# Linear attention with a mixture of experts: the queries projected transposed, for two chunks at once

## What is computed

```
h = _layernorm(x, axis=-1) * (1 + ca) + sa
q = _heads(x @ wq.T);  k = _heads(x @ wk.T);  v = _heads(x @ wv.T)
def _phi(x, omega):
    proj = jnp.einsum('bhnd,md->bhnm', x, omega)
    norm = 0.5 * jnp.sum(x * x, axis=-1, keepdims=True)
    return jnp.exp(proj - norm) / math.sqrt(M)
kv_cumsum = jnp.cumsum(jnp.einsum('bhnm,bhnd->bhnmd', phi_k, v), axis=2)
out = jnp.einsum('bhnm,bhnmd->bhnd', phi_q, kv_cumsum)
z = 1.0 / (jnp.einsum('bhnm,bhnm->bhn', phi_q, k_cumsum) + 1e-06)
x = x + ga * ((out * z[..., None]) @ wo.T + bo)
x = x + gb * ffn(_layernorm(x) * (1 + cb) + sb)
```

## Time and profile before

| | |
|---|---|
| three runs | 727.18, 728.42, 729.02 us; median 728.42 |
| the profiled execution | 727.18 us, its span 725.1 us |
| TensorE (PE) busy | 697.4 us, 96% |
| VectorE (DVE) busy | 536.0 us, 74% |
| ScalarE (ACT) busy | 387.6 us, 53% |
| GpSimd (POOL) busy | 335.6 us, 46% |

### The profile page before, as it was taken

The page is one execution under the profiler, slowest core; times in us unless marked ns, Lnnn a source line. Parts: engine busy times, 40 slices in busy tenths (PEclk is TensorE's granted clock), DMA queues, the critical chain, the costliest instruction groups (busy, mean ns, idle before and its releaser), DMA issues. The chain is left out here.

```text
span 725.1 us, 27349 instructions
## 1 busy us (share of the span) xinstructions
PE 697.4 (96%) x11452; PEld 604.1 (83%) x11452; DVE 536.0 (74%) x1685; ACT 387.6 (53%) x740; POOL 335.6 (46%) x625
## 2 busy tenths in 40 slices
PE   8999999999999999999999999999999789999956
PEld 8788888888888888888888888888887779999942
DVE  6687888878878887888878878888775456565416
ACT  5755566665656665666656566665552144544310
POOL 3002545555544445454545554545447306556550
PEclk9999999999999999999999999999999999999989
DMA  9974000000000000000000000000000154553128
GB/s 252 362 268 178 11 9 11 10 9 11 14 15 10 11 10 11 10 10 11 9 11 11 14 14 9 11 11 11 10 11 14 49 177 130 168 173 113 51 82 304
DMA packets 32705, 47.25 MB, mean 65 GB/s; under 512 B 4132, under 2 KB 20168, under 8 KB 32584
## 3 DMA queue, kind: packets, MB, share of 16 engines
q1 hardware_dynamic: 23296, 32.62, 13.4%
q0 software_dynamic: 4096, 8.42, 3.6%
q10 hardware_dynamic: 5192, 4.47, 1.9%
HBM read 22.21 MB, written 23.36 MB: 63 GB/s over the span
## 5 line engine op out<-in xcount | busy, mean ns | idle before, releaser
L1297 POOL DMA_INDIRECT y_rows<-y_sb,row_id x64 | 62.8, 982 | 66.0 <-DVE y_sb L1442 49.9
L1108 POOL DMA_INDIRECT dispatched<-h_cur,slot x64 | 67.3, 1051 | 17.8 <-issue 16.1
L1376 ACT ACTIVATE hidden<-bank,b_col 128x512 f32<-128x512 f32 x64 | 43.3, 689 | 58.2 <-PE bank L1348 57.8
L632 ACT ACTIVATE phi_k<-expo_k 128x1024 f32<-128x1024 f32 x32 | 33.9, 1058 | 74.5 <-DVE expo_k L768 70.7
L648 ACT COPY v_sb<-bank 128x512 f32<-128x512 f32 x64 | 37.6, 587 | 62.1 <-PE bank L279 58.7
L527 PEld LDWEIGHTS bank<-woT,attT 128*128 128x128 f32 x512 | 61.9, 192 | 3.2 <-ACT attT L738 0.6
L859 DVE TENSOR_TENSOR scores<-bank,within 128x512 f32<-128x512 f32 x64 | 41.2, 686 | 31.2 <-PE bank L310 31.2
L527 PE MATMUL bank<-woT,attT 128*128 128x128 f32 x512 | 62.4, 275 | 0.4 <-ACT attT L738 0.4
L1317 PE MATMUL bank<-w_sb,hidden 128*128 128x128 f32 x512 | 59.7, 275 | 0.8 <-issue 0.8
L137 POOL TENSOR_TENSOR rs<-var,power 128x1 f32<-128x1 f32 x64 | 37.1, 579 | 49.8 <-DVE var L132 49.5
L1317 PEld LDWEIGHTS bank<-w_sb,hidden 128*128 128x128 f32 x512 | 58.3, 192 | 1.2 <-issue 1.2
(11 more groups left out here) (243 smaller groups left out, 2037.9 us busy)
## 6 DMA issues: line engine op xcount, KB each, us to landing
dispatched<-blank SPq DMA_DIRECT2D x16, 524.0 KB, 3.1
region<-dispatched SPq DMA_DIRECT2D x30, 262.0 KB, 2.9
y_rows<-blank SPq DMA_DIRECT2D x8, 512.0 KB, 3.9
w_nat<-in_L_ffn_w_dram SPq DMA_DIRECT2D x8, 256.0 KB, 3.7
y_got<-y_rows SPq DMA_DIRECT2D x8, 256.0 KB, 6.8
y_got<-y_rows ACTq DMA_DIRECT2D x8, 256.0 KB, 7.4
out_dram<-x_sb SPq DMA_DIRECT2D x8, 256.0 KB, 3.7
w_sb<-in_L_ffn_w_dram ACTq DMA_DIRECT2D x6, 256.0 KB, 2.8
```

The source lines that it names most:

```text
L1108: pool.indirect_dma_start(out=dispatched[:, :], in_=h2_cur[par][:], in_offset=None, out_offset=bass.IndirectOffsetOnAxis(ap=slot[par][:, k ...
L1297: pool.indirect_dma_start(out=y_rows[:, :], out_offset=bass.IndirectOffsetOnAxis(ap=row_id[par][:, t:t + 1].bitcast(U32), axis=0), in_=y_s ...
L1376: act.activation(hidden[par][:, k, :], psum[2 + k][:], ACT.Gelu, bias=b1_col[:, bass.ds(e * KH + k, 1)]).then_inc(sem(f"hid{k}_out"), 1)
```

## The change

The queries are no longer projected by rows and then transposed. `project_qT` makes them transposed at once: the weights of two heads are held in the array and the tokens of two chunks, 256 columns, are streamed past them. A pair of chunks needs this for 8 pairs of heads; one step does half of it, two steps ahead. `exponent_qT` then makes the exponent on TensorE: omega times the queries plus -0.5 times their squares, as 16 fp32 matmuls of 64 by 64 by 256 columns on the four quadrants, summed in PSUM. ScalarE takes the exponential straight into `phiT_q`. The weight pq, q's squares on ScalarE, their sum and the two exponents on VectorE and the transposes of phi_q go; VectorE squares the transposed queries (`square_q`, 128x1024). The scale of 1/8 that both features had is now 1/64 on the keys.

```
-            if front:
-                pe.wait_ge(sem("h_split"), c + 2)
+            if c:
+                features_T(1, c, par)
+                features_T(0, c, par)
+            if live(c, 2):
+                project_qT(c + 2)
             if front:
-                project("q0", c, nxt)
-                project("q1", c, nxt)
-            features_T("tq0", c, par)
...
+                project("k0", c)
+                project("k1", c)
+                project("v0", c)
+                project("v1", c)
+                project("pk0", c)
+                project("pk1", c)
             if tail:
                 attend_state(1, c - 1, nxt, (j - 1) % CPB)
             state_gain(0, c, par, j)
             if tail:
                 attend(1, c - 1, nxt, (j - 1) % CPB)
-            if front:
-                project("v0", c, nxt)
-                project("v1", c, nxt)
+            if live(c, 2):
+                exponent_qT(c + 2, c)
             score(0, c, par)
             score(1, c, par)
...
+def project_qT(n):
+    first = 2 * (n % 2)
+    pair = n // 2
+    hi, lo = h_hi[pair % 3][:, :, 0, :], h_lo[pair % 3][:, :, 0:P]
...
+    for side in range(2):
...
+        for i in range(2):
+            o = q_bank(side, n)[:, i * 2 * P:(i + 1) * 2 * P].rearrange("p (c t) -> p c t", t=P)
+            cols = slice(side * 512 + (first + i) * P, side * 512 + (first + i + 1) * P)
+            pe.matmul(o, wT_hi["q"][:, cols], hi, start=True, stop=False)
+            pe.matmul(o, wT_lo["q"][:, cols], hi, start=False, stop=False)
+            mm = pe.matmul(o, wT_hi["q"][:, cols], lo, start=False, stop=True)
+        mm.then_inc(sem(f"q{side}_in"), 1)
+def exponent_qT(n, c):
...
+    for i in range(2):
+        for w, of in ((omT, queries_of(n)), (minus_half, squares_of(n))):
+            for side in range(2):
+                for r in range(2):
...
+                    mm = pe.matmul(q_bank(r, n)[half_rows(side), i * 2 * P:(i + 1) * 2 * P],
+                                   w[half_rows(r), :], of[half_rows(r), cols],
+                                   start=(w is omT), stop=(w is minus_half), skip_group_check=True)
```

More of the change, by code:

```diff
@@ L273, in project @@
                             cols = slice(half * 512, (half + 1) * 512)
-                            first = HALF if half and w in ("k", "pk", "v") else 0
+                            first = HALF if half else 0
                             toks = slice(first, first + P)
-                            pe.matmul(o, twice(h_hi[par])[:, toks], wT_hi[w][:, cols], start=True, stop=False)
-                            pe.matmul(o, twice(h_hi[par])[:, toks], wT_lo[w][:, cols], start=False, stop=False)
-                            pe.matmul(o, h_lo[par][:, toks], wT_hi[w][:, cols], start=False, stop=True).then_inc(sem(kind + "_in"), 1)
@@ L281, in features_T @@
[L281 to L293, removed]
+                            pe.matmul(bank[:], hi_of(n)[:, toks], wT_hi[w][:, cols], start=True, stop=False)
@@ new lines, in project, with features_T @@
+                            pe.matmul(bank[:], hi_of(n)[:, toks], wT_lo[w][:, cols], start=False, stop=False)
+                            pe.matmul(bank[:], lo_of(n)[:, toks], wT_hi[w][:, cols], start=False, stop=True).then_inc(sem(kind + "_in"), 1)
+                        def features_T(half, c, par):
+                            if c >= 2:
+                                pe.wait_ge(sem("attT1_out" if half else "wo_out"), c - 1)
+                            elif c == 1:
+                                pe.wait_ge(sem(f"a{half}_out"), 1)
+                            pe.wait_ge(sem("phi_k_ready"), c + 1)
@@ L337, in attend @@
                         def attend(g, c, par, j):
-                            if g == 0:
-                                for z in range(2):
-                                    pe.wait_ge(sem(f"a{z}_out"), c + 1)
+                            if g == 0 and c == 0:
+                                pe.wait_ge(sem("a1_out"), 1)
                             pe.wait_ge(sem("o_begun"), 2 * c + g + 1)
@@ L385, in attended_T @@
                                 pe.wait_ge(sem(f"a{half}_out"), c + 1)
+                            elif not half:
+                                pe.wait_ge(sem("wo_out"), c - 1)
                             for j in range(4):
@@ L710, in rows_out, with heads_out @@
                                 act.copy(h2T[:], psum[BANK["h2T"]][:, 0:P]).then_inc(sem("h2T_out"), 1)
+                            def heads_out():
+                                for half in range(2):
+                                    act.wait_ge(sem(f"attT{half}_in"), c)
+                                    act.copy(attT[:, half * 4:half * 4 + 4, :].rearrange("p a b -> p (a b)"),
+                                             psum[BANK[f"attT{half}"]][:]).then_inc(sem(f"attT{half}_out"), 1)
                             def logits_out():
```

499 lines of the change are left out of this document (270 added, 229 removed), and 4 rows, old and new, of the table TURNS.

## The result

The changed kernel took 738.44 us (median of four runs, 734.44 to 739.54), the kernel before 727.80 beside it: a ratio of 1.0137, with a 95% interval of 1.0115 to 1.0159. It is slower by 1.4%. Said were 732.5 us within 720 to 742; the direction and the range hold, but the loss is 10.6 us where the forecast had 4.8 on the profiled execution.

The account below looks back on a forecast made before the run. TensorE, busy 96% of the span, was taken as the bound. Full steps 0, opening +4.5, step 30 -2.2, step 31 +2.5 gave +4.8 on the profiled 727.18 (732.0); said 732.5 us, range 720 to 742.

Parts of the forecast that it names:

- The removed and added work of a step: TensorE in a full step: 4.16 us of work removed, 3.27 added, so its own work falls by 0.89.
- The mask's wait: Full step, `attended_T` after the scores: waits for VectorE's mask once pq no longer stands between; 0.8 us new idle a step.
- `wo_out`: Keys' first half waits for VectorE's read of the bank that `add_heads` fills: 0.1 us a step (0 to 0.2).
- The slow stretch: First block of quadrant matmuls in a step takes 1.80 us, the second 1.57; the extra 0.23 was kept as unchanged.
- the rival: Full steps get faster: the first quadrant block loses its extra 0.23, 29 x 0.23 = 6.7 us less, 725.8; chance 0.28.
- 0 + 4.5 - 2.2 + 2.5: Whole kernel: full steps 0, opening +4.5, step 30 -2.2, step 31 with the next chunk's row +2.5; sum +4.8 us.
- The opening: Start to step 1: +4.5 us, from q's new work, waits for mask and state (0.6 each), and norming more chunks.
- Step 30: Step without q: 3.27 us of work given back, less about 1.1 of new waiting; -2.2 us.
- The keys' wait: Step 30: k comes right behind the transposed keys and waits for ScalarE's two copies of them, about 1.1 us.
- Step 31: Step without projections: 2 us longer as the routed row comes late; the next chunk's row adds about 0.5; +2.5 us.
- The late row: Step 31: with GpSimd's scatter ahead, the routed row comes about 2.9 us later; TensorE waits some 4 us.
- The rival of the clock: Every step: the new pause lets TensorE's clock fall to 1.2 GHz, 46 us more, 778; chance 0.01.

## Why the prediction was right or wrong

**The removed and added work of a step: right.** Removed were 4.16, from the two timelines it is 4.17 (q and pq 2.93, the transposes 0.92, the three kept projections 0.32). Added were 3.27, now 1.52 and 1.72 = 3.24. The 0.12 for a matmul of 256 columns and 1.74 for `exponent_qT` hold to 0.02.

**The mask's wait: right.** Forecast 0.8. The first of the heads' transposes starts 0.96 behind the routed row's transpose, where the forecast had 0.89, and 0.17 if nothing were waited for: 0.79 more, of which 0.63 is idle. The second half never waits. `wo_out`, priced at 0.1, shows no wait in any full step.

**The slow stretch: wrong step of the sum.** "I keep the 0.23 as it is": it went, in the 19 of 28 steps that had it, and 0.11 more, as the block is now followed by small matmuls (1.45, not 1.56). The reason given to the rival, what stands ahead of the block, is not shown, and why the stretch came and went is open. Against it stand 0.19 that `add_heads` costs more in its new place ahead of the rank (1.89, before 1.70) and 0.11 for the transpose at the step's head. So a step fell by 0.145 on the mean, and by 0.21 in the two that were read, where 0 was said. The rival's 6.7 counted the stretch in all 29 steps, which was too much as well.

**Late packets: the step of the working that failed.** The sum "0 + 4.5 - 2.2 + 2.5" has no term for TensorE's instruction stream. The change put 28 matmuls, 16 of them in two passes, in place of 20 that had one, and pushed the small ones closer together; the trace of before had the warning, one idle row of 0.8 that ended in "issue". It cost 5.9 in the full steps and 1.1 in step 30, more than half of the whole loss. (The 5.9 is all that the eight longer steps lost beyond the one of before; in each of the eight a packet was entered 2.3 to 2.8 us behind the start of its transfer. That the denser order is what made packets late is argued from the run with v ahead of the block, not isolated.) The Trainium skill ("Runtime: NRT & Kernel Launch", section on instruction fetch mechanics) describes a queue refilled in blocks of 256 instructions, and calls the cost of crossing one mostly hidden: the 256 agree with the 97 packets here, the hiding does not where a packet's instructions run off in 2 us.

**The opening: right in kind.** +3.8 for +4.5; its two new waits were 0.46 and 0.35 where 0.6 each was said.

**Step 30: -0.2, not -2.2.** The keys' wait was as priced, 1.07 more on the way from their transposes to k. Not in the sum were the mask, for which TensorE idled 1.49, since VectorE ends the divisions and the state (543.24) after TensorE goes on from the scores (542.16), and a late packet (0.80 idle, `add_heads` 1.1 longer).

**Step 31: +4.7 alone, where 2.5 was for it and the chunk behind it.** The late row was right, 4.71 for "some 4 us"; the clock behind it was not priced, and took 2.2 (5.22 to `add_heads` where the run with the scatter put back took 3.03 at full clock). The rival of the clock had been given 0.01 and a place in every step; it came in this one place, after 7 us in which TensorE was busy for 2.40. In the full steps, with a pause of 0.63 each, the page's clock row stays at 9 throughout. By the Trainium skill's rule of the second failure mode ("TensorE: Matmul & The Clock Gate") those pauses would have lowered it; no row shows that.

So the side was right, with errors that partly cancelled. Against the forecast's 4.8 stand: -0.7 in the opening, -4.1 in the steps, +7.0 by late packets, +0.9 in step 30 beside its packet, +3.5 at the end: 11.4. That all but the late packets comes to 4.4, near the forecast, is luck: -4.8 and +4.4 of errors that have nothing to do with one another. That the time lies inside the range is partly luck for the same reason.

## What to carry to other kernels

Count the instructions of a dense stretch as well as its columns: several hundred small matmuls in a row can outrun the loading of the stream, and such idle time ends in nothing a profile names. When work moves away from behind a producer's last read, half of it may be enough as cover, and the other half can keep two dense stretches apart. In the last steps, where no other work is left, look at each wait again, and at the clock behind it. And when a block's time is taken from one step, read the same block in the other steps before it goes into a sum 29 times.

## What the runs showed of the hardware

- TensorE's instructions come in packets of 256 (97 transfers of 16 KB). Counted through all eleven traces from 20 to 575 us, no packet was entered sooner than 2.18 us after its own transfer had begun; and from 60 to 540 us every idle stretch of over 0.1 us that ends in "issue" ends at a packet's first instructions, 2.2 to 3.1 us after that transfer began. Why some transfers begin about 0.8 after the packet before is entered and others about 3 after it was not found.
- A block of 96 small fp32 products takes 1.45 where more of its kind follow and 1.56 where `routing_rank` or `add_heads` does. Ahead of a 512-column projection it took 1.56 to 1.60 or 1.79 to 1.81, and nothing here tells why.
- Waits that are already fulfilled follow one another 0.106 us apart on TensorE; among its long matmuls 45 of them cost a step 0.17.
- After 4.71 us of idle time, in a stretch of 7 us in which TensorE was busy for 2.40, the clock was at half for the next 5.3 us. After 2.14 or 2.15 us at the same place it stayed whole in two runs and went to half in three, for part of the way to `add_heads` (0.74, 0.66 and 0.72 on the mean). Behind step 30's wait of 1.49 for the mask it differs too: whole in the changed kernel, at half from 535.9 to 539.3 with the whole product behind the scores and the steps filled. What decides is not shown.
